# Silu through the hyperbolic tangent, reciprocal roots from the bits of the number, and another order of the lead and of the weights' remaking

## The reference

```python
x = x + conv(ln(x))        # q,k,v projections; softmax of k and v over the 256 tokens;
                           # descriptors = einsum(q, softmax k); out = descriptors x softmax v, times Wr, plus br
t = x as 4096 tokens
logits = ln(t) @ Wg        # 8 experts; the best two, softmax weights
h = ln(t) @ W1[e];  g = ln(t) @ W3[e] + b3[e]
t = t + sum over the two experts of weight * (silu(h) * g) @ W2[e]
```

## Time and profile before

| what | value |
|---|---|
| median of 3 runs (lowest to highest) | 305.33 us (304.55 to 306.17) |
| the profiled execution, own time | 306.4 us |
| its span, first to last instruction | 304.7 us |
| TensorE's mean granted clock in it | 0.912 of full speed |
| busy: PE, DVE, ACT, POOL | 252.5, 163.8, 169.7, 133.7 us |
| from the start to the first transpose of a slot's rows | 89.5 us |
| slots inside steps 4 to 8 | 89.5 to about 209 us |
| the slots alone | about 209 to 285 us |
| results added and stored | the rest |

### The profile page before, as it was taken

One profiled execution on the slowest core, in us unless ns is written; L12 is line 12 of the kernel. 1 busy time (PEld: TensorE's weight loads), 2 busy tenths in 40 slices (PEclk: granted clock), 3 DMA queues, 4 the chain that ended last, 5 costly groups with the idle time before them and its releaser, 6 DMA issues.

```text
span 304.7 us, 6569 instructions
## 1 busy us (share of the span) xinstructions
PE 252.5 (83%) x1602; PEld 210.9 (69%) x1602; DVE 163.8 (54%) x753; ACT 169.7 (56%) x484; POOL 133.7 (44%) x150
## 2 busy tenths in 40 slices
PE   7769797979549998988996995999998999999200
PEld 3446463636248987967996985989998999999100
DVE  4462868586845755484573457347343343434542
ACT  2636164837438679648767744765565656565200
POOL 4000007372712753772577377267753264435400
PEclk9557999799958999999998899899999999999955
DMA  4789101010112410113331011233333222018188
GB/s 121 260 241 311 44 2 45 26 55 17 54 44 66 114 47 18 54 53 86 85 88 44 28 53 58 78 103 90 105 99 87 56 73 61 28 36 295 41 264 289
DMA packets 31737, 28.33 MB, mean 93 GB/s; under 512 B 5147, under 2 KB 29541, under 8 KB 31701
## 3 DMA queue, kind: packets, MB, share of 16 engines
q1 hardware_dynamic: 24608, 16.82, 19.8%
q0 software_dynamic: 4320, 8.92, 8.8%
q10 hardware_dynamic: 2772, 2.17, 2.1%
HBM read 15.89 MB, written 12.01 MB: 92 GB/s over the span
## 4 chain that ended last, share of the span: by engine, by line
PE 56%; DVE 15%; ACT 9%; issue 8%; DMA 6%; POOL 3%; SPq 1%; DVEq 0%; ACTq 0%; POOLq 0%
PE bank L681 12%; PE bank L671 7%; PE bank L655 6%; PE bank L656 6%; PE bank L657 6%; DMA both<-result_rows 3%; PE bank L650 2%; POOL sorted_rows L1395 2%; PE bank L588 2%; PE bank L643 2%; ACT L944 2%; PE bank L560 2%; PE bank L543 2%; ACT row_buf L873 2%; PE bank L597 1%
## 5 line engine op out<-in xcount | busy, mean ns | idle before, releaser
L1395 POOL DMA_INDIRECT sorted_rows<-row_buf,position x64 | 61.6, 963 | 89.6 <-ACT row_buf L873 51.0
L1402 POOL DMA_INDIRECT result_rows<-ys,xs x71 | 68.4, 963 | 63.3 <-ACT ys L919 48.0
L1273 DVE TENSOR_TENSOR xs_lo<-bank,xs_hi 128x128 fp32r<-128x128 f32 x71 | 20.6, 290 | 84.6 <-ACT xs_hi L902 82.9
L681 PE MATMUL bank<-w_down,act_t 128*128 x426 | 60.7, 280 | 1.5 <-ACT act_t L912 1.5
L919 ACT ACTIVATE ys<-bank,xs 128x128 f32<-128x128 f32 x71 | 26.1, 368 | 59.6 <-PE bank L681 58.7
L681 PEld LDWEIGHTS bank<-w_down,act_t 128*128 128x128 f32 x426 | 54.4, 196 | 1.9 <-issue 1.9
L655 PE MATMUL bank<-w_up,xs_hi 128*128 x142 | 54.9, 387 | 0.0
L656 PE MATMUL bank<-w_up,xs_lo 128*128 x142 | 48.5, 342 | 0.0
L657 PE MATMUL bank<-w_up,xs_hi 128*128 x142 | 48.4, 341 | 0.0
L671 PE MATMUL bank<-ident,act_rows 128*128 128x128 f32 x213 | 36.3, 280 | 8.1 <-ACT act_t L912 6.1
L1280 DVE TENSOR_TENSOR act_rows<-both,bank 128x384 f32<-128x384 f32 x71 | 38.9, 548 | 4.6 <-ACT both L907 1.8
(11 more groups left out here) (166 smaller groups left out, 347.0 us busy)
## 6 DMA issues: line engine op xcount, KB each, us to landing
xs<-sorted_rows SPq DMA_DIRECT2D x71, 65.0 KB, 1.9
both<-result_rows SPq DMA_DIRECT2D x16, 256.0 KB, 4.4
x_all<-x_dram SPq DMA_DIRECT2D x8, 256.0 KB, 3.4
out_dram<-both ACTq DMA_DIRECT2D x8, 256.0 KB, 4.1
both<-L_ffn_W_dram SPq DMA_DIRECT2D x2, 960.0 KB, 9.1
w_down<-L_ffn_W_dram SPq DMA_DIRECT2D x3, 512.0 KB, 10.7
both<-L_ffn_W_dram SPq DMA_DIRECT2D x2, 576.0 KB, 5.3
result_rows<-ys,xs POOLq DMA_INDIRECT x71, 2.2
```

Of the source, the lines that this page charges most:

```text
L681: last = nc.tensor.matmul(bank[4][:, 0:C], act_t[s.par][:, k * P:(k + 1) * P], w_down[:, ds(e, 1), k * C:(k + 1) * C].rearrange("p a c -> ...
L1395: nc.gpsimd.indirect_dma_start(out=sorted_rows.ap(), out_offset=bass.IndirectOffsetOnAxis(ap=position[u.par][:, c:c + 1], axis=0), in_=row ...
L1402: nc.gpsimd.indirect_dma_start(out=result_rows.ap(), out_offset=bass.IndirectOffsetOnAxis(ap=xs[s.ring][:].bitcast(I32)[:, DEST:DEST + 1], ...
```

## The change

Five things are changed. Silu becomes a tanh on ScalarE (h times one half inside) and one VectorE instruction more, `twice_silu`, (tanh + 1) * h, which is twice the silu; the factor of two goes out with the rows' weights (`gap_den` is doubled). The tanh lies in one table set with the exponential, and ScalarE loads that set once, in step 4. From unit 6 on (step 4 on) the first guess of the reciprocal root comes from the bits of the number on VectorE: a shift, a multiply-add and two Newton steps, eight instructions in `find_shift` that wait for each other, in place of the logarithm and exponential on ScalarE. In PE `up(s, 0)` now waits for `silu_ready` of s-1. The row of b3 is no longer added by a third matmul: its high and low part are written into w_up by 16 DMAs of SP, each pair behind `split_up` of its expert. And in the lead steps the order is another one: the root comes ahead of `copy_pk`, `transpose_probs` moves to the end of the step before, the sums are inverted earlier, `remake_up` is cut in two halves placed apart, `split_up` of the `end` expert is done earlier, `logits_of_x` comes behind `weigh_tokens` (in all steps), and eight `keep_busy` matmuls are added in step -2.

```diff
+            sp.wait_ge(b3_hi_ready, 1)
+            sp.wait_ge(b3_lo_ready, 1)
+            for e in range(E):
+                sp.wait_ge(up_lo_ready, e + 1)
+                for half, part in enumerate((b3_hi, b3_lo)):
+                    sp.dma_start(w_up[:].bitcast(F32)[P - 1:P, e, 1, half, :],
+                                 part[:].bitcast(F32)[e:e + 1, :]).then_inc(b3_rows_in, 16)
...
-            def remake_up(e):
+            def remake_up(e, j):
+                last = nc.tensor.matmul(up_banks(e)[j][:, 0:F], elim[:], w_raw[:, e, j, :], start=True, stop=True)
...
# PE turn
+                    pe.wait_ge(b3_rows_in, 16 * 2 * E)
+                if 0 < s.n <= FINAL:
+                    pe.wait_ge(silu_ready, s.n)
# PE iteration
-                if exists(i):
+                if exists(i) and i.n >= FIRST_STEP:
                     transpose_probs(i)
-                if exists(new):
-                    logits_of_x(new)
...
                 if exists(i):
                     weigh_tokens(i)
+                if exists(new):
+                    logits_of_x(new)
+                    keep_busy(5, bank[4])          # step -2
+                if middle is not None:
+                    at_least(pe, up_lo_ready, middle - 1)
                     keep_busy(4)
+                    remake_up(middle, 0)
                 mix_channels(i)
+                if middle is not None:
                     keep_busy(3)
+                    remake_up(middle, 1)
...
-                if middle is not None:
-                    remake_up(middle)
                 if exists(later):
                     transpose_xn(later)
+                if exists(new) and new.n < FIRST_STEP:
+                    transpose_probs(new)
+                if i.n == -2:
+                    keep_busy(3, bank[4])
+                if end is not None and i.n >= 0:
+                    remake_up(end, 0)
...
+                if i.n == -1:
+                    weights_product()
+                    remake_up(end, 0)
                 if end is not None:
-                    remake_up(end)
+                    remake_up(end, 1)
# ACT
-                nc.scalar.activation(silu_h[s.par][:], h_of(s), ACT.Silu).then_inc(silu_ready, 1)
+                nc.scalar.activation(silu_h[s.par][:], h_of(s), ACT.Tanh, scale=0.5).then_inc(tanh_ready, 1)
+                if has_norms(later) and i.n < FIRST_STEP:
+                    rough_rstd(later)
                 if exists(i):
                     copy_pk(i)
-                if i.n > FIRST_STEP:
-                    nc.scalar.preload_act_table_set("natural_log_exp_and_others")
-                if has_norms(later):
-                    rough_rstd(later)
+                if i.n == FIRST_STEP:
+                    nc.scalar.preload_act_table_set("exp_and_others")
-                if i.n >= FIRST_STEP:
-                    nc.scalar.preload_act_table_set("silu_and_others")
                 copy_xk(i)
+                if before is not None:
+                    round_weights(before)
...
                     normalise_probs(new)
+                if middle is not None:
+                    round_weights(middle)
# DVE
+            def guess_rstd(m):
+                after(tensor_single_scalar(half_bits, var_eps as int32, 1, arith_shift_right))
+                after(tensor_scalar(rough as int32, half_bits, -1.0, 0x5F3759DF, mult, add))
+                for k in range(2):                      # three chained instructions each
+                    newton[0] = var_eps * -0.5 * last;  newton[1] = newton[0] * last
+                    better[k] = (newton[1] + 1.5) * last;  last = better[k]
+            def twice_silu(s):
+                dve.wait_ge(tanh_ready, s.n + 1)
+                nc.vector.scalar_tensor_tensor(out=silu_h[s.par][:], in0=silu_h[s.par][:], scalar=1.0, in1=h_of(s),
+                                               op0=ALU.add, op1=ALU.mult).then_inc(silu_ready, 1)
                 if s.has(0):
+                    twice_silu(s)
                     gated(s)
...
# DVE iteration: invert_sums(new) ahead of weigh_and_place(old), scale_x_logits(new) behind it;
# split_up(before) behind stats_of_x in turn 4, split_up(middle) alone at the end of the step
```

More of the change, by code:

```diff
@@ L155, in build @@
         rough = sb("rough", [P, 2, TPU])
+        half_bits = sb("half_bits", [P, 2, TPU], I32)
+        better = [sb(f"better{i}", [P, 2, TPU]) for i in range(2)]
         newton = [sb(f"newton{i}", [P, 2, TPU]) for i in range(2)]
@@ L624, in rank @@
                 last.then_inc(rank_ps, 1)
-            def remake_up(e):
[L630 to L637, removed]
+            def remake_up(e, j):
+                if j == 0:
+                    pe.wait_ge(early_in if e < LOADED_FIRST else late_in, EXPERT_LOADS)
+                    pe.wait_ge(elim_ready, 1)
+                    at_least(pe, up_lo_ready, e - 1)
+                last = nc.tensor.matmul(up_banks(e)[j][:, 0:F], elim[:], w_raw[:, e, j, :], start=True, stop=True)
+                if j == 1:
+                    last.then_inc(up_ps, 1)
             def keep_busy(n, o=bank[7]):
@@ L931, in turn @@
                 if s.has(0):
-                    silu(s)
+                    tanh_h(s)
                 if s.has(1) and s.n < FINAL:
@@ L1065, in add_eps @@
                 nc.vector.tensor_tensor(var_eps[:], mean_var[:, :, :, 1], eps[:], ALU.add).then_inc(var_ready, 1)
-            def find_shift(m):
-                dve.wait_ge(rough_ready, m.n + 1)
-                after(nc.vector.scalar_tensor_tensor(out=newton[0][:], in0=var_eps[:], scalar=-0.5, in1=rough[:],
+            def guess_rstd(m):
+                steps = 8 * (m.n - FIRST_STEP - 2)
+                dve.wait_ge(var_ready, m.n + 1)
+                after(nc.vector.tensor_single_scalar(half_bits[:], var_eps[:].bitcast(I32), 1, ALU.arith_shift_right),
+                      guess_steps, steps + 1)
+                after(nc.vector.tensor_scalar(rough[:].bitcast(I32), half_bits[:], -1.0, float(0x5F3759DF),
+                                              ALU.mult, ALU.add), guess_steps, steps + 2)
+                last = rough
+                for k in range(2):
+                    after(nc.vector.scalar_tensor_tensor(out=newton[0][:], in0=var_eps[:], scalar=-0.5, in1=last[:],
+                                                         op0=ALU.mult, op1=ALU.mult), guess_steps, steps + 3 * k + 3)
+                    after(nc.vector.tensor_tensor(newton[1][:], newton[0][:], last[:], ALU.mult),
+                          guess_steps, steps + 3 * k + 4)
+                    after(nc.vector.scalar_tensor_tensor(out=better[k][:], in0=newton[1][:], scalar=1.5, in1=last[:],
+                                                         op0=ALU.add, op1=ALU.mult), guess_steps, steps + 3 * k + 5)
+                    last = better[k]
+                return last
@@ L1072, in find_shift @@
+            def find_shift(m):
+                guess = rough
+                if m.n < FIRST_STEP + 2:
+                    dve.wait_ge(rough_ready, m.n + 1)
+                else:
+                    guess = guess_rstd(m)
+                after(nc.vector.scalar_tensor_tensor(out=newton[0][:], in0=var_eps[:], scalar=-0.5, in1=guess[:],
                                                      op0=ALU.mult, op1=ALU.mult), newton_steps, m.n * 3 + 1)
-                after(nc.vector.tensor_tensor(newton[1][:], newton[0][:], rough[:], ALU.mult),
+                after(nc.vector.tensor_tensor(newton[1][:], newton[0][:], guess[:], ALU.mult),
@@ L1074, in find_shift @@
                       newton_steps, m.n * 3 + 2)
                 wait_norms(dve, m)
-                after(nc.vector.scalar_tensor_tensor(out=rstd[:], in0=newton[1][:], scalar=1.5, in1=rough[:],
+                after(nc.vector.scalar_tensor_tensor(out=rstd[:], in0=newton[1][:], scalar=1.5, in1=guess[:],
                                                      op0=ALU.add, op1=ALU.mult), newton_steps, m.n * 3 + 3)
@@ L1306, in iteration @@
                 if exists(new):
+                    invert_sums(new)
+                turn(slot_of_turn(i, 2))
+                if exists(old):
+                    weigh_and_place(old)
+                if exists(new):
                     scale_x_logits(new)
                 if i.n == -1:
+                    convert_consts()
                     stats_of_x(i.shift(3))
                     add_eps(i.shift(3))
[L1311 to L1315, removed]
                     split_br()
-                if exists(old):
-                    weigh_and_place(old)
+                    split_b3()
                 turn(slot_of_turn(i, 3))
@@ L1324, in iteration @@
                     stats_of_x(i.shift(3))
+                if before is not None:
+                    split_up(before)
                 turn(slot_of_turn(i, 5))
@@ L1346, in iteration @@
                     choose_experts(i)
-                for e in (before, middle):
-                    if e is not None:
```

(3 more changed lines are left out.)

43 lines of the change are left out of this document (23 added, 20 removed).

## The result

The changed kernel takes **315.50 us** (315.28 to 315.99, three runs) against 305.33 before: ratio 1.0335, 95% interval 1.029 to 1.038. It is slower by 10 us where I had forecast 1.5 less. Its profiled execution has a span of 314.3 us (before 304.7), so 9.6 us are to be found in the trace.

What follows compares the result with a forecast made beforehand. It saw no engine full in the lead, where VectorE waits for itself around three engines, and later slots at TensorE's pace. Lead -9.4 plus slots +7.9 gave -1.5, so 303.8 us against the median of 305.33; range 298.0 to 308.8.

Steps and rivals of the forecast that it cites:

- Start, -4.0: Start of the lead: earlier inversion, a dropped matmul pair and `keep_busy` holding the clock up gain 4.0 us (1.4 to 5.4).
- Steps 1 and 2, 12.5 each: Lead steps 1 and 2: VectorE's 1.84 us root wait goes, leaving 12.5 us each; 5.0 gained, less 0.6 for lower clock.
- Step 3, -1.0, and from scatter to slot, 14.2: Lead's end: unit 2's rows come 1.0 us earlier in step 3; first scatter to first slot takes 14.2 us.
- The 16 DMAs at nothing: SP's queue ahead of `load_rows`: the small DMAs cost nothing, covered by eight scatters; rival that they show, +3, chance 0.05.
- Logits, +1.1: First slot: `logits_of_x` of unit 5 leaves TensorE's idle time and follows the first slot's transpose in view, costing 1.1 us.
- Table loads, -0.6: Heads of steps 5 to 8: one load for nine, against VectorE's guess chain and new product, gains 0.6 us.
- the 0.85: Step 7: the clock fall after TensorE's 2.44 us wait has a 60% chance to go, gaining 0.85 us.
- One more instruction per slot, +2.7: Slot turns of steps 4 to 8: the loop becomes 2.29 us against 2.15; 2.7 us lost in all (1.5 to 4).
- the late chains, +5.1: Turns where table and norms fill VectorE: 1.6 us each in steps 5 and 7, 0.9 in 6 and 8; 5.1 lost.
- VectorE as a bound of the mixed steps: Rival, table chain and step heads of steps 5 and 7: TensorE's stops add clock falls of 1.4 each; 308.5 us, chance 0.21.
- the lead pays more: Rival, lead and slots: the lead gains 11.4 us and slots lose only 5, giving 299 us; chance 0.26.
- The loads in full: Rival, heads of steps: eight loads of 1.28 us come fully off the path, giving 294 us; chance 0.05.

Runs made afterwards that it cites:

- e4: The changed kernel run once more with nothing altered: 315.50 us (313.07 to 318.27).
- e1: The changed kernel with Silu, logarithm, exponential and nine table loads put back, so only the order stays changed: 302.12 us, ratio 0.989 to the kernel before.
- e3: The changed kernel with transposed rows in the bank of g and `twice_silu` ahead of `xs_lo` on VectorE: 303.41 us, ratio 0.997 to the kernel before.
- e13: The changed kernel plus unread matmuls, five in step -1 and four in each of steps 1 to 3: 308.23 us, ratio 1.010 to the kernel before.
- e9: The changed kernel with `logits_of_x` of unit 5 back in TensorE's idle time before the first slot: median 313.98 us.
- e5: The changed kernel without `twice_silu` and its wait, the gate's product taking the tanh itself: 296.77 us, ratio 0.973 to the kernel before.
- e10: The kernel before with only the lead's order changed, and `logits_of_x` of unit 5 in the idle time before the first slot: 298.62 us, ratio 0.975.
- e12: The changed kernel with rows in the bank of g, `twice_silu` first, `logits_of_x` of unit 5 in the idle time: 304.97 us, ratio 0.996 to the kernel before.

## Why the prediction was wrong, point by point

The sum was -9.4 + 7.9; the trace has -3.8 and +13.4. Of the 11.1 us between, 5.6 are in the lead's term and 5.5 in the slots'.

*Start, -4.0.* Measured -0.1 in this execution. The step that failed is the one that let the eight `keep_busy` hold the clock up: the clock fell at 14 us and stayed down to 31. The low end of 1.4 was not low enough, since I had priced the two halves of the remake ahead of the attention at 0.88 each, and neither the logits, which move to the same place, nor the lower clock. In e4, the same kernel, step 1 opens at 36.9, in e1 and e3 at 34.1 and 34.3, 4 us earlier: the mechanism was right, its condition was not given.

*Steps 1 and 2, 12.5 each.* Step 1 took 12.60, and e13's steps 12.54 and 12.33: right. Step 2 took 14.87, with the clock down from 51 to 58 (0.57 in its window) and VectorE standing 2.10 us for TensorE's mixing; I had put 0.6 aside for such a stretch, it cost 2.4. That VectorE stands only for the root was true of step 1 before; in step 2 it also stood 1.00 us for the same mixing.

*Step 3, -1.0, and from scatter to slot, 14.2.* 71.47 - 65.57 = 5.90, 1.3 less than before; 14.29. Right.

*The 16 DMAs at nothing.* Right. The last of them and the first slot's load, from SP's queue in the changed kernel:

```profile
80.87 0.50 SPq L472 DMA_DIRECT2D w_up<-b_hi  x1
81.41 0.59 SPq L472 DMA_DIRECT2D w_up<-b_lo  x1
83.65 6.38 SPq L486 DMA_DIRECT2D xs<-sorted_rows  x6
```

They are issued 1.65 us before the load, which waits for the scatters.

*Logits, +1.1.* The first product now follows the first slot's rows by 6.51 in place of 4.30: +2.2. Of this 1.7 are the logits, as e9 shows, and 0.5 is the second product ahead of the first. At the lower clock the eight matmuls take 1.82, and I had taken a value between two clocks, although the trace of before has the lower one there, from 83.9 on.

*Table loads, -0.6.* The heads have -0.74 (+0.07, +0.15, -0.74 and -0.22, where I had +0.2, +0.2, -0.8 and -0.2): right, and by the working given. At the head of step 5 the chain of the guess is there link by link:

```profile
112.01 0.17 DVE L1101 TENSOR_SCALAR rough<-half_bits 128x8 int32<-128x8 int32 x1
112.22 0.17 DVE L1105 SCALAR_TENSOR_TENSOR newton<-var_eps,rough 128x8 f32<-128x8 f32 x1
...
114.50 0.21 ACT L926 ACTIVATE gap_exp<-gap_scaled 128x4 f32<-128x4 f32 x1 [1.54 <-DVE gap_scaled L1199]
...
115.49 0.52 PE L685 MATMUL bank<-ident,act_rows 128*128 128x128 f32 x3 [1.67 <-ACT act_t L942]
```

0.21 a link, ScalarE waiting for VectorE, and TensorE standing 1.67 us (1.53 in the earlier trace rows). The fall of the clock in step 7 did go in this execution, but that was luck: e4, the same kernel, has it there behind a stop of 1.60 (0.50 from 171.2 to 174.2), where this one stopped for 1.62. A fall behind the stop in step 5 came in its place (0.50 from 116 to 119), which the 0.85 had not foreseen; e4 has none there.

*One more instruction per slot, +2.7, and the late chains, +5.1, less the 0.85 of the clock.* Measured 12.4, of which e5 gives 11.8 to the second product and the wait on it. Two terms were mis-sized. The loop is 2.48, not 2.29: I had put the next h right behind the second product, but in `turn` the wait for `silu_ready` stands ahead of `transpose_rows`, so the rows' transpose and its handing over are in the loop. And the second product costs 0.60 on average in every turn in which VectorE was full. I counted two such turns in steps 5 and 7 and one in 6 and 8, 5.1 us; the trace has three in each of steps 5, 6 and 7, two in step 8 and one in step 4, 7.2 us (the rows from 159 us on show one). It could have been read in the trace of before by following VectorE alone. The other turns hold 5.2 in place of 2.7 less 0.85; 1.0 of it is the first turn, which e1 and e5 have too and e10, with the logits in the idle time, has not.

*The rivals.* VectorE as a bound of the mixed steps is what happened, but not for the reason I gave it (falls of the clock): its own queue is enough. I had priced it at 308.5 by adding clock falls to the forecast's 7.9, so that the range ended below the truth. That it should decide only from two falls on was wrong too. That the lead pays more came true only in e13, with seventeen further unread matmuls. The loads in full (8 x 1.28 = 10.2, not the 10.3 I wrote) are not seen: 3.3 in e5.

## What to carry to other kernels

Before giving an engine one more instruction in every turn, add up its queue turn by turn: in the turns where it had no gap, one of 0.55 us cost 0.60 on average here, and where it had one of 0.7 it cost nothing, whatever the engine's share of the span said. A wait that stands in a queue ahead of more than needs it makes all that lies between part of the loop. And price each part of a lead at both clock levels: the same instructions gained 0.1 or 4 us at its start.

## What the runs showed of the hardware

Seventeen unread matmuls in two kinds of gap kept the granted clock at 1.00 from 10 to 64 us of e13's lead (0.78 in the changed kernel); they took 7 us from the changed kernel and about 3 from e10. Without them, the same instructions were granted 0.50 from 14 or 15 us to 22, 28 or 31, from one execution to another.

The length of a stop alone did not decide whether the clock fell behind it. The first stop of TensorE at the head of step 5, and the window behind it, in e4 and in e12:

```profile
114.15 0.52 PE L685 MATMUL bank<-ident,act_rows 128*128 128x128 f32 x3 [1.65 <-ACT act_t L942]
115.00:118.00 3.00, 2.90 (x20) 1.00 0.07 22
...
107.26 0.52 PE L685 MATMUL bank<-ident,act_rows 128*128 128x128 f32 x3 [1.29 <-ACT act_t L946]
109.00:112.00 3.00, 3.00 (x12) 0.50 0.13 44
```

A stop of 1.65 us left the clock alone in e4, one of 1.29 was followed by 0.50 for 3 us in e12, and one of 1.67 by the same in the changed kernel.
